# Starting the max pass one chunk step sooner and folding the null key into its last reduce, in a gated cross-attention and mixture-of-experts kernel

## The reference, cut to what matters

```python
xn, cn = _ln(x, ln1_s, ln1_b), _ln(context, lnc_s, lnc_b)
q = xn @ Wq;  k, v = jnp.split(cn @ Wkv, 2, axis=-1)
k = concatenate((null_k, k));  v = concatenate((null_v, v))
sim = einsum('bhid,bhjd->bhij', q * h ** -0.5, k)
attn = softmax(where(mask, sim, -max))
out = _ln((attn @ v) @ Wo, lno_s, lno_b)
x = x + tanh(g_xattn) * out
x = x + tanh(g_ffn) * moe(_layernorm(x))      # eight experts, one chosen per token
```

## Time and profile before

| what | us |
|---|---|
| median of 3 runs (769.25 to 772.37) | 771.68 |
| the profiled execution's own time | 773.45 |
| its span | 771.6 |
| TensorE busy | 700.4 (91%) |
| VectorE busy | 618.1 (80%) |
| ScalarE busy | 494.3 (64%) |
| GpSimd busy | 384.2 (50%) |

### The profile page before, as it was taken

One profiled execution on the slowest core, in us unless ns is written; L12 is line 12 of the kernel. 1 busy time (PEld: TensorE's weight loads), 2 busy tenths in 40 slices (PEclk: granted clock), 3 DMA queues, 4 the chain that ended last, 5 costly groups with the idle time before them and its releaser, 6 DMA issues.

```text
span 771.6 us, 14853 instructions
## 1 busy us (share of the span) xinstructions
PE 700.4 (91%) x5041; PEld 394.5 (51%) x5041; DVE 618.1 (80%) x1079; ACT 494.3 (64%) x635; POOL 384.2 (50%) x429
## 2 busy tenths in 40 slices
PE   2798989789989998999899989999999899999997
PEld 2554444445444544454445444544454445468886
DVE  4875969696979697969796979698969695887776
ACT  1316575647576767666766676668566766777885
POOL 6745846744636363636363636364726316466200
PEclk9759999999999999999999999999999999999999
DMA  5803051412212211222122212122220201000000
GB/s 160 175 28 71 11 105 57 98 57 45 69 27 77 42 63 31 74 41 64 31 74 41 64 31 74 38 67 43 63 41 24 42 25 56 24 26 2 1 14 14
DMA packets 73993, 40.34 MB, mean 52 GB/s; under 512 B 61309, under 2 KB 68501, under 8 KB 73957
## 3 DMA queue, kind: packets, MB, share of 16 engines
q1 hardware_dynamic: 73525, 39.77, 20.7%
q10 hardware_dynamic: 432, 0.10, 0.1%
HBM read 26.65 MB, written 0.52 MB: 35 GB/s over the span
## 4 chain that ended last, share of the span: by engine, by line
PE 61%; DVE 14%; ACT 10%; issue 6%; DMA 4%; POOL 3%; SPq 1%; ACTq 0%; DVEq 0%; POOLq 0%
PE S L1178 19%; PE A L1198 17%; PE X L1237 10%; ACT S L646 5%; ACT PP L651 4%; PE S L1336 4%; DVE PP L916 3%; PE A L1353 3%; DVE mneg L985 3%; DMA zTh<-z_hi 2%; DVE mx L964 2%; DMA raw<-ctx_dram 1%; PE X L1353 1%; PE X L1247 1%; PE A L1125 1%
## 5 line engine op out<-in xcount | busy, mean ns | idle before, releaser
L646 ACT ACTIVATE S<-S,mb 125x896 f32<-125x896 f32 x192 | 187.6, 977 | 179.7 <-PE S L1178 179.7
L916 DVE TENSOR_TENSOR PP<-S,PP 125x896 f16<-125x896 f32 x192 | 209.1, 1089 | 90.2 <-ACT PP L651 87.5
L964 DVE TENSOR_REDUCE mx<-X 128x1 f32<-128x500 f32 x336 | 211.8, 670 | 10.6 <-PE X L1237 8.8
L1198 PE MATMUL A<-PP,z_hi 125*128 125x448 f16 x768 | 209.4, 354 | 1.7 <-DVE Af L948 1.5
L651 ACT ACTIVATE PP<-S 125x896 f16<-125x896 f32 x192 | 175.1, 912 | 4.9
L1237 PE MATMUL X<-zTh,qh 128*128 128x500 f16 x336 | 135.3, 408 | 19.1 <-DVE mx L964 11.2
L1198 PE MATMUL A<-PP,z_lo 125*128 125x448 f16 x384 | 122.0, 354 | 0.0
L1178 PE MATMUL S<-qh,zTh 128*128 128x448 f16 x384 | 104.2, 353 | 9.7 <-DVE PP L916 9.6
L1198 PEld LDWEIGHTS A<-PP,z_hi 125*128 125x128 f16 x768 | 73.6, 98 | 75.0 <-DVE Af L948 5.2
L1178 PE MATMUL S<-qh,zTl 128*128 128x448 f16 x384 | 104.0, 353 | 0.0
L1178 PE MATMUL S<-ql,zTh 128*128 128x448 f16 x384 | 104.0, 353 | 0.0
(11 more groups left out here) (201 smaller groups left out, 1232.2 us busy)
## 6 DMA issues: line engine op xcount, KB each, us to landing
raw<-ctx_dram SPq DMA_DIRECT2D x16, 750.0 KB
Rb<-r_scratch SPq DMA_DIRECT2D x16, 448.0 KB, 3.6
wst<-in_w_dram SPq DMA_DIRECT2D x16, 256.0 KB, 3.8
early<-in_Wkv_dram SPq DMA_DIRECT2D x2, 512.0 KB, 14.2
early<-in_Wq_dram SPq DMA_DIRECT2D x1, 512.0 KB, 5.7
Wo_s<-in_Wo_dram SPq DMA_DIRECT2D x1, 512.0 KB, 11.6
zTh<-z_hi SPq DMA_TRANSPOSE x32, 2.8
zTl<-z_lo SPq DMA_TRANSPOSE x32, 2.8
```

Of the source, the lines that this page charges most:

```text
L646: act.activation(s, s, ACT.Exp, bias=mb[:, p, c:c + 1]).then_inc(e_done, 1)
L916: dve.tensor_tensor(Pl[:, k, :].rearrange("p (a r) -> p a r", a=2), S[0:CK, 2 * (c % 2):2 * (c % 2) + 2, 0:HR], Ph[:, k, :].rearrange("p ( ...
L964: dve.reduce_max(mx3[:, t, blk:blk + 1], X[:, j % 2, 0:KB], AX).then_inc(mx_red, 1)
L1198: ins = mm(A[:, a, 0:HR], z[:, p, c, :], q[:, k, a * HR:(a + 1) * HR], start=(c == 0 and n < 2), stop=(c == NC - 1 and n >= 4))
```

## The change

- The 21 maxima matmuls, their reduces and waits move from steps 2 to 8 to steps 1 to 7; the seven small transposing matmuls move from step 9 to step 8. In the first body the projections' value steps 14 and 15 move along.
- The array of maxima has a fourth column. At step 3 VectorE writes minus the null key's term into it (a tensor_scalar from a contiguous row of 7 into every fourth element). One tensor_reduce at step 7, behind the 21st reduce and ahead of `sub`, yields `mneg` in fp16. The separate minimum is gone. A constant (SHIFT - 2) moves into the mask's bias by one more instruction in the prologue.
- `t7` is made by GpSimd behind `normalise`, and its exponential by ScalarE in step 2 of the following body, with a bias. `null7` has two buffers, and `move_null` waits for the `t7` of one batch earlier.
- `context_stats` of steps 0 and 1 is one run of six in step 0.

```diff
--- before.py
+++ after.py
@@ -105,10 +105,9 @@
         tmp2 = sb("tmp2", [CK, NC])
         mhalf = sb("mhalf", [128, NC])
         nullrow = sb("nullrow", [1, R])
-        null7 = sb("null7", [128, RT])
-        null7s = sb("null7s", [128, RT])
-        mx3 = sb("mx3", [128, RT, 3])
-        negm = sb("negm", [128, RT])
+        null7 = sb("null7", [128, 2, RT])
+        mx4 = sb("mx4", [128, RT, 4])
+        shift0 = sb("shift0", [128, 1])
         mneg = sb("mneg", [128, RT], fp16)
         t7 = sb("t7", [128, RT])
         P07 = sb("P07", [128, 2, RT])
@@ -356,9 +355,9 @@
 
             wait_ge = waiter(sp, sp_gate)
 
-            def move_null(n):
+            def move_null(n, p):
                 wait_ge(null_done, 2 * n + 2)
-                sp.dma_start(null7[:, :], nullrow[0:1, :].rearrange("o (r t) -> o r t", t=RT)).then_inc(null_in, 16)
+                sp.dma_start(null7[:, p, :], nullrow[0:1, :].rearrange("o (r t) -> o r t", t=RT)).then_inc(null_in, 16)
 
             def turn(p, half):
 
@@ -392,8 +391,9 @@
                         wait_ge(an_done, b - 1)
                     sp.dma_start(Rb[:, :], r_dram[0:1, :].partition_broadcast(128)).then_inc(rb_in, 16)
                 if f["znext"]:
-                    wait_ge(t7_done, b + 2)
-                    move_null(b + 2)
+                    if f["main"]:
+                        wait_ge(t7_done, b + 1)
+                    move_null(b + 2, p)
                 for e in f["wload"]:
                     load_expert(e)
 
@@ -401,7 +401,7 @@
             turn(0, 0)
             sp.wait_ge(split2_done, 1)
             turn(0, 1)
-            move_null(0)
+            move_null(0, 0)
             iterate(sp, body, B - 4)
             b = B
             sp.wait_ge(a_copied, b)
@@ -483,6 +483,7 @@
 
 
             ch.link(pool.memset(mhalf[:, :], -0.5))
+            ch.link(pool.memset(shift0[:, :], SHIFT - 1.0))
             ch.link(pool.memset(z_hi[96:128], 0.0))
             ch.link(pool.memset(z_lo[96:128], 0.0))
             pool.memset(zl[:, :, :, 0:1], 0.0)
@@ -548,6 +549,11 @@
                     if f["b_ge2"] and p == 1:
                         wait_ge(y_ready, b - 1)
                     normalise(1 - p)
+                if f["prep"]:
+                    wait_ge(mneg_done, b + 2)
+                    if f["prev"]:
+                        wait_ge(p0_done, b + 1)
+                    pool.tensor_tensor(t7[:, :], mneg[:, :], null7[:, 1 - p, :], ALU.subtract).then_inc(t7_done, 1)
                 for e in f["wexp"]:
                     split_expert(e)
 
@@ -703,6 +709,8 @@
                         act.activation(b1T[:, :], A[:, 1, 0:E * FC], ACT.Copy).then_inc(b1_copied, 1)
                     if c == 10 and f["znext"] and not queries_early:
                         queries(b + 2, p, 0)
+                    if c == 2 and f["main"]:
+                        null_weight(b, p)
                     if f["group"] and c == 9:
                         xt_copy(2, 1.0, 0.0)
 
@@ -712,8 +720,11 @@
                 act.activation(qh[0:1, np_, :].rearrange("o (r t) -> o r t", t=RT),
                                X[0:1, :, :].rearrange("o a r -> o (a r)")[:, 0:R]
                                .rearrange("o (t r) -> o r t", t=RT), ACT.Copy).then_inc(slot_done, 1)
-                act.wait_ge(t7_done, nb + 1)
-                act.activation(P07[:, np_, :], t7[:, :], ACT.Exp).then_inc(p0_done, 1)
+
+            def null_weight(b, p):
+
+                act.wait_ge(t7_done, b + 1)
+                act.activation(P07[:, p, :], t7[:, :], ACT.Exp, bias=shift0[:, 0:1]).then_inc(p0_done, 1)
 
 
             value_copy(0)
@@ -810,6 +821,7 @@
                 dve.wait_ge(ld_m, 16)
                 ch.link(dve.tensor_copy(maskf[:, :, :], mask_s[:, :, :]))
                 ch.link(dve.tensor_scalar(mbias[:, :, :], maskf[:, :, :], 1.0, MASK_BIAS, ALU.subtract, ALU.mult))
+                ch.link(dve.tensor_scalar(mbias[:, :, :], mbias[:, :, :], SHIFT - 2.0, None, ALU.add))
                 dve.tensor_scalar(mcol[:, :, :], maskf[:, :, :], 1.0 - MASKED, MASKED, ALU.mult,
                                   ALU.add).then_inc(mask_ready, 1)
 
@@ -961,34 +973,27 @@
 
                 blk, t = divmod(j, RT)
                 dve.wait_ge(mx_ready, NMX * nb + j + 1)
-                dve.reduce_max(mx3[:, t, blk:blk + 1], X[:, j % 2, 0:KB], AX).then_inc(mx_red, 1)
+                dve.reduce_max(mx4[:, t, blk:blk + 1], X[:, j % 2, 0:KB], AX).then_inc(mx_red, 1)
 
             def body(b, p, f):
                 nb, np_ = b + 1, 1 - p
                 for c in range(NC):
-                    j0 = 3 * (c - 2)
-                    maxima = f["prep"] and 2 <= c <= 8
+                    j0 = 3 * (c - 1)
+                    maxima = f["prep"] and 1 <= c <= 7
                     if maxima and c == 3:
 
-
                         dve.wait_ge(null_in, 16 * (nb + 1))
-                        dve.tensor_scalar(null7s[:, :], null7[:, :], SHIFT - 1.0, None, ALU.add).then_inc(ns_done, 1)
+                        dve.tensor_scalar(mx4[:, :, 3], null7[:, np_, :], -1.0, -1.0, ALU.mult, ALU.add).then_inc(ns_done, 1)
                     if maxima:
                         reduce(nb, j0)
                         reduce(nb, j0 + 1)
-                    if maxima and c == 8:
+                    if maxima and c == 7:
                         reduce(nb, j0 + 2)
-                    if c == 9 and f["prep"]:
                         dve.wait_ge(mx_red, NMX * (nb + 1))
                         dve.wait_ge(ns_done, nb + 1)
-                        ch.link(dve.tensor_reduce(negm[:, :], mx3[:, :, :], AX, ALU.max, negate=True))
-                        dve.scalar_tensor_tensor(mneg[:, :], negm[:, :], SHIFT - 2.0, null7s[:, :], ALU.add,
-                                                 ALU.min).then_inc(mneg_done, 1)
-                        dve.wait_ge(mneg_done, nb + 1)
                         if f["prev"]:
-                            dve.wait_ge(p0_done, nb)
-                        dve.scalar_tensor_tensor(t7[:, :], mneg[:, :], 1.0, null7[:, :], ALU.add,
-                                                 ALU.subtract).then_inc(t7_done, 1)
+                            dve.wait_ge(t7_done, nb)
+                        dve.tensor_reduce(mneg[:, :], mx4[:, :, :], AX, ALU.max, negate=True).then_inc(mneg_done, 1)
                     if c == NC - 1 and f["main"] and f["prep"]:
                         a_copy(b, f["tail"])
                     late = c == 10 and not f["y"]
@@ -1001,11 +1006,10 @@
                         sub(*ahead(b, c))
                     if f["znext"] and late:
                         queries(b + 2, p, c - 10)
-                    if maxima and c < 8:
+                    if maxima and c < 7:
                         reduce(nb, j0 + 2)
-                    if c < 2 and f["main"]:
-                        if f["znext"]:
-                            context_stats(b + 2, p, range(HC + 3 * c, HC + 3 * c + 3), None)
+                    if c == 0 and f["main"] and f["znext"]:
+                        context_stats(b + 2, p, range(HC, NC), None)
                     if f["group"]:
                         if c == 0:
                             dve.wait_ge(y_done, NT)
@@ -1028,7 +1032,7 @@
             queries(0, 0, 1, S[:, 2:4, :])
             for b in (-1, 0, 1):
                 body(b, b % 2, flags(b))
-            n0, PER = ch.n, 1 + 1
+            n0, PER = ch.n, 1
             with dve.Fori(2, B - 5, 2) as i:
                 ch.base, ch.n = PER * i - 2 * PER + n0, 0
                 body(i, 0, STEADY[0])
@@ -1218,8 +1222,8 @@
             def aux(b, p, c, part, f):
 
                 nb, np_ = b + 1, 1 - p
-                if 2 <= c <= 8:
-                    j = 3 * (c - 2) + part
+                if 1 <= c <= 7:
+                    j = 3 * (c - 1) + part
                     blk, t = divmod(j, RT)
                     if j < 2:
                         if j == 0:
@@ -1238,10 +1242,10 @@
                        zTh[:, np_, blk * KC:(blk + 1) * KC, 0:CK], start=True, stop=True).then_inc(mx_ready, 1)
                     if not f["main"] and j % 2:
                         value_step(4 + j // 2)
-                if c == 9 and not f["main"] and part == 1:
+                if c == 8 and not f["main"] and part == 1:
                     value_step(14)
                     value_step(15)
-                if c == 9 and part == 2:
+                if c == 8 and part == 2:
                     pe.wait_ge(mneg_done, nb + 1)
                     for t in range(RT):
                         ins = mm(X[0:1, t // 4, (t % 4) * 128:(t % 4 + 1) * 128], mneg[:, t:t + 1], idh[:, :],
```

## The result

| what | us |
|---|---|
| before, median of 4 (769.25 to 772.37) | 771.01 |
| after, median of 4 (795.24 to 798.54) | 797.12 |
| ratio, 95% interval | 1.034 (1.030 to 1.038) |
| after, the profiled execution's own time, and its span | 798.54, 796.7 |
| TensorE busy, after | 711.4 (89%) |

The change makes the kernel slower by 26 us. The forecast was 773.1 with a range to 790, so it was wrong, and the range too.

What follows compares the result with a forecast made beforehand. TensorE (busy 91%) was taken as the bound, its idle time being what could be won. -18.0 - 12.9 + 19.0 + 12.8 + 0.3 + 0.2 = +1.4 us: 774.9 profiled, 773.1 median; range 759 to 790.

Steps and rivals of the forecast that it cites:

- Part 4: Null column's tensor_scalar at step 3: escapes GpSimd's `centre`, by 0.17 us in odd bodies, under a tenth in even; +0.3 us.
- Rival 1: Null column at step 3 collides with `centre`: 781.6 us if in five even bodies, 791.8 in all eleven; chance 0.33.
- Part 2: Maxima in step 1: TensorE waits there for the first reduce (odd bodies) or late transposed z (even); +19.0 us.
- Part 1, second term: Steps from sim(5) to sim(11): five with maxima and one bare step replace six with maxima; -12.9 us over 15 bodies.
- The first term: Sim(11) to next sim(0): transposes move to step 8, one reduce makes `mneg`, its stall goes; -18.0 us over 15 bodies.
- Part 3: L924, add of row sums, collides with GpSimd's two-input L467 in bodies 3 to 13; +12.8 us, bounds 0 and 16.
- Part 5: The rest: `t7` on GpSimd, its exponential and `move_null` cost nothing more; prologue's mask instruction +0.2 us, bounds -0.2 and +0.6.

Runs made afterwards that it cites:

- the fold alone: Changed kernel with maxima, transposes and statistics put back in their old steps, leaving the fourth column, single reduce and GpSimd's `t7`: 757.52 us, ratio 0.982.
- both cures, loads moved: Changed kernel with null column at step 1, reciprocals at step 6, loads of experts 2 to 5 behind the transposes of bodies 1 and 13: 754.98 us.

## Why the prediction was wrong

**Part 4 failed, in both its numbers.** It put the null column ahead of `centre` in even bodies by less than a tenth and took "no collision" as likeliest. The margin was the difference of two sums of several durations each. sim(4) came 1.83 behind the landing of z, not 1.77, and sub(4) 3.38 behind sim(4), not 3.30. These 0.14 are most of what turned the order in bodies 4, 6, 8 and 10, which it did by 0.11 to 0.20; body 12, where the wait for z was 0.42 and not 0.85, kept it by 0.05. Odd bodies kept it by 0.13, forecast 0.17. The price was 1.7 a body and is 4.0: the earlier trace rows held a block during which TensorE still had work, and no fall of the clock. Four blocks of 4.0 are 16 of the 24 us missed. Rival 1 named this mechanism and its place, with a chance of 0.33, as high as the forecast's own. With its own bodies (five even ones) it gave 781.6; four bodies at 4.0 put on the forecast are 789.2. The upper end of the range, 790, stood on the same 1.7.

The Trainium skill ("SBUF — State Buffer", section "Who interferes with whom") counts tensor_scalar among the instructions that can contend with GpSimd for the shared ports, where its operands allow the modes that use both. The traces agree: 2.67 against 0.16 here with a strided result, 2.71 with a contiguous one. The prediction cited it and then let the margin of a tenth decide. By the same section of the Trainium skill a tensor_reduce never contends on this chip. In the kernel after this is not put to the test, since GpSimd runs nothing while `mneg` is made. With the fold alone it is: 0.18 or 0.19 in the 12 bodies where GpSimd was at work.

**Part 2, bodies 1 and 2.** Forecast +2.9 and +1.5, measured +5.4 and +4.0. Their waits for z in step 1 were 4.62 and 5.07, and the clock read 0.62 and 0.63 behind them (155.6 to 163.0 above). The prediction added the step that no longer hides the transfer and left out the clock, though the window 151.5 to 154.6 of before showed it at 0.55. How much of the difference is the clock and how much the longer wait, no run parts. The other bodies cost 14.9 us, forecast 14.6 (odd +1.34 for +1.28, even +1.0 for +0.95). These 5 us are the second part of the miss.

**Part 1, second term.** From sim(5) to sim(11), with collisions and the moved transposes taken out, the gain is 9.4 us and not 12.9: a body wins 0.6 to 0.7, not 0.83 (which over 15 bodies is 12.4; the 12.9 was 0.5 too much as a sum already): with the transposes taken out the bare step came to 2.35 (2.84 - 0.49), not 2.27, and even bodies have a first step of 3.24 there (sim(5) to sim(6) with the null column free), not 3.12. **The first term** (-18.0) was right to a tenth, **Part 3** to 0.2 (+12.6 for +12.8): L936 at 1.51 in odd bodies and 1.31 in the even ones from 4 to 10, ending with L467. **Part 5** was small, as said.

The sum: 1.4 as forecast, +15.7 for the null column, +5.3 for the step 1 of bodies 1 and 2 mainly, +3.5 for the second term of Part 1, -0.9 for the rest, is 25.0, and the spans differ by 25.1.

## What to carry to other kernels

A race that an argument decides by less than the scatter of the durations it is summed from has no likelier side: price it at its full cost in the forecast, and in the kernel take it out, by moving the short instruction a step away or making it a form that can't be held (here 14 us for a `3` that becomes a `1`, and 14 for a `5` that becomes a `6`). Then look for the race at the new place: of the four traces with the column at step 1, two have it held in body -1, and TensorE waits 5.3 us there and not 2. Before the price of a stall is taken from an existing one, see in the windows what TensorE did during it and at what clock it ran afterwards. And when a wait is moved ahead, look at what it used to hide: the fold wins 14 us by itself, and the move that came with it lost 40.

## What the runs showed of the hardware

- Behind a block in which TensorE was busy 0.59 of 2.70 us the granted clock averaged 0.64 over the next 4.8 us, and a step of 2.95 took 4.6. Behind one with 1.50 busy in 3.10 (body 2 of the kernel before) it stayed at 1.00. Behind one of four like blocks of the kernel with the reciprocals at step 6 it also stayed at 1.00 (a step of 2.95), and no run here says why.
- With ten useless matmuls (2.06 us) in each such block the clock stayed at 1.00 in bodies 4, 6, 8 and 10. The step behind took 1.64 less and the body 1.44 less, in one execution of one kernel.
- A tensor_scalar of 7 elements a partition is held by a GpSimd tensor_tensor of 2.75 us if it comes 0.11 behind it, and takes 0.16 if it comes 0.05 ahead (body 12: 569.12 against 569.17).
- A transposing DMA that lands in 2.8 us keeps TensorE waiting 5.07 when it is queued among weight loads (DMA share 0.99 over 149.2 to 155.5); with the loads behind it (both cures, loads moved), the wait in the same body is 0.57.
